# First norm's factor applied to the outputs of the query, key and value projections, inputs split without it, eight PSUM banks in that stage

## The reference, cut to what matters

```
x = rms_norm(hidden_states, ln_in_w)          # w * (x * rsqrt(mean(x*x) + 1e-6))
mixed = jnp.where(vm, x @ v_qkv, x @ l_qkv)   # vm: per token, which of two experts
q, k, v = jnp.split(mixed, 3, axis=-1)
q, k = apply_rotary(q, k, position_ids, l)
ctx = sdpa(q, k, v, causal=True)              # 16 heads of 32
```

## Time and profile before

| | |
|---|---|
| median of 3 runs | 2036.79 us (2032.74 to 2040.6) |
| profiled execution, its own time | 2036.72 us |
| its span, first to last instruction | 2034.9 us |
| granted TensorE clock, mean | 0.977 |
| PE busy | 1918.8 us, 94% |
| DVE, ACT, POOL busy | 1113.8, 830.2, 887.1 us |
| PE's first matmul / first product of the projections | 18.38 / 26.22 us |
| first scores of the self-attention | 138.29 us |

### The profile page before, as it was taken

One profiled execution on the slowest core, in us unless ns is written; L12 is line 12 of the kernel. 1 busy time (PEld: TensorE's weight loads), 2 busy tenths in 40 slices (PEclk: granted clock), 3 DMA queues, 4 the chain that ended last, 5 costly groups with the idle time before them and its releaser, 6 DMA issues.

```text
span 2034.9 us, 35472 instructions
## 1 busy us (share of the span) xinstructions
PE 1918.8 (94%) x12620; PEld 1642.6 (81%) x12620; DVE 1113.8 (55%) x2663; ACT 830.2 (41%) x2198; POOL 887.1 (44%) x1037
## 2 busy tenths in 40 slices
PE   4999979997999999999999999998979999999998
PEld 3876767775999989888899879985458888887997
DVE  6777875666442553547676554222384766655422
ACT  2017526875211211256666423222235666652321
POOL 3340322341798999641121348840044212104884
PEclk9999988999999999999999999998989999999999
DMA  3110100010233333310000213322221000001332
GB/s 127 42 57 2 40 15 16 30 50 17 83 109 109 115 114 124 88 35 18 11 24 13 67 63 104 114 73 88 70 80 34 19 10 24 13 1 42 104 113 79
DMA packets 38190, 118.88 MB, mean 58 GB/s; under 512 B 6168, under 2 KB 10264, under 8 KB 38016
## 3 DMA queue, kind: packets, MB, share of 16 engines
q1 hardware_dynamic: 31408, 107.92, 17.3%
q10 hardware_dynamic: 6608, 8.68, 1.4%
HBM read 114.75 MB, written 1.84 MB: 57 GB/s over the span
## 4 chain that ended last, share of the span: by engine, by line
PE 82%; DVE 7%; POOL 5%; ACT 2%; issue 2%; DMA 1%; DVEq 0%; ACTq 0%; SPq 0%; POOLq 0%
PE psum L565 15%; PE psum L566 14%; PE psum L567 14%; PE psum L787 7%; PE psum L798 6%; PE psum L845 5%; PE psum L558 4%; PE psum L685 4%; PE psum L687 4%; PE psum L686 4%; POOL wl L1701 3%; DVE xc L1277 1%; DVE rstd L1262 1%; ACT probs_t L1042 1%; DVE total L1248 1%
## 5 line engine op out<-in xcount | busy, mean ns | idle before, releaser
L1701 POOL TENSOR_TENSOR wl<-raw,wh 128x256 fp32r<-128x256 f32 x656 | 518.9, 822 | 13.7
L565 PE MATMUL psum<-nh,wh 128*128 128x448 f32 x904 | 348.3, 385 | 15.3 <-DVEq L1477 8.0
L1693 POOL TENSOR_SCALAR wh<-raw 128x1024 fp32r<-128x1024 f32 x164 | 185.1, 1129 | 396.8 <-PE psum L567 158.4
L566 PE MATMUL psum<-nl,wh 128*128 128x448 f32 x904 | 336.9, 373 | 0.0
L567 PE MATMUL psum<-nh,wl 128*128 128x448 f32 x904 | 336.3, 372 | 0.0
L1042 ACT ACTIVATE probs_t<-masked_t,nmin 112x375 f32<-112x375 f32 (+1 forms) x384 | 202.6, 529 | 109.2 <-DVE nmin L1380 109.2
L1549 DVE TENSOR_TENSOR hid_l<-scr,hid_h 128x448 fp32r<-128x448 f32 x108 | 93.2, 863 | 229.0 <-ACT hid_h L1129 228.4
L565 PEld LDWEIGHTS psum<-nh,wh 128*128 128x128 f32 x904 | 174.7, 193 | 37.6 <-issue 12.5
L1380 DVE CUSTOM_DVE_ANT_0 masked_t<-psum,maskf 112x375 f32<-112x375 f32 x256 | 129.7, 544 | 116.9 <-PE psum L787 116.2
L798 PE MATMUL psum<-cst,probs_t 112*125 112x112 f32 (+1 forms) x1304 | 188.4, 274 | 3.8 <-ACT probsT_t L1069 3.4
L1069 ACT COPY probsT_t<-psum 125x336 f32<-125x336 f32 (+1 forms) x424 | 175.5, 456 | 40.4 <-PE psum L845 23.4
(11 more groups left out here) (182 smaller groups left out, 3861.9 us busy)
## 6 DMA issues: line engine op xcount, KB each, us to landing
raw<-in_walls SPq DMA_DIRECT2D x183, 512.0 KB, 3.5
raw<-in_ctxF SPq DMA_DIRECT2D x24, 375.0 KB, 3.0
ctxb<-in_ctxF ACTq DMA_DIRECT2D x8, 375.0 KB, 3.6
ctxt<-in_ctxK ACTq DMA_DIRECT2D x8, 375.0 KB
x<-in_xT ACTq DMA_DIRECT2D x2, 896.0 KB, 11.2
outT<-x SPq DMA_DIRECT2D x2, 896.0 KB, 5.1
mask<-in_kmask ACTq DMA_DIRECT2D x16, 41.0 KB, 2.6
vself<-in_tt SPq DMA_DIRECT2D x1, 448.0 KB, 6.5
```

The lines of the kernel that those rows point to most:

```text
L565: nc.tensor.matmul(out, ah, bh, start=(i == 0), stop=False)
L566: nc.tensor.matmul(out, ah, bl, start=False, stop=False)
L1693: nc.gpsimd.tensor_scalar(high, src, 1.0, 1.0, ALU.mult, ALU.mult).then_inc(split_h, 1)
L1701: last = nc.gpsimd.tensor_tensor(low[cut], src[cut], high[cut].bitcast(F32), ALU.subtract)
```

## The change

1. The norm of this block no longer scales its input. New parts "x" (`X_PART`): for each slice ACT writes `nh_` as x*w, rounded, and squares x; DVE writes `nl_` as x*w - nh_ and adds the square to `total`. The products can start from these.
2. The factor, once its reciprocal is there, is multiplied into the masks: `vr0` (mask times factor, per expert) is used in `part_of` in place of `vm`, `vml` for queries and keys. For the values the factor is needed with tokens in partitions: four small matmuls per half with two columns (`total` times `mean_w`), a root into `std_t`, a reciprocal, and `vmT` is multiplied by it.
3. Order: half 0's part "x" comes first on ACT and DVE, ahead of positions, tables and token types; its variance and the tables come behind the first tile, half 1's part "x" behind them and its variance behind the second tile.
4. The stage has eight banks (`plan.use(range(8))`), the rotations lag by two tiles and have a counter of their own ("rope"); before the attention PE waits for the last readers of banks 3 to 7, and goes back to three.
5. Loads: the first weights are issued first on SP; the second half of x is issued once the first has landed; the waits for the constants move from the start of PE and GpSimd to where they are used.

```diff
+        vr0 = at("vr0", [P, 2, T], F32, o_k)
...
-            "qk": [("norm", 0, 0, "s"), ("norm", 0, 0, "v"), ("table",), ("norm", 0, 0, "f")] + qk_order(parts(0, 1, s=(0, 0, 0), v=(0, 0, 1), f=(0, 0, 1))),
+            "qk": [("norm", 0, 0, "x"), ("norm", 0, 0, "f")] +
+            qk_order(both({(0, 0, 0): [("norm", 0, 0, "v"), ("table",)]}, parts(0, 1, x=(0, 0, 0), v=(0, 0, 1), f=(0, 0, 1)))),
...
+                    pe.wait_ge(cst_in, 16)
-                    nc.tensor.matmul(pool_bank(n)[:, 0:HALF], mean_w, total[:, :], start=True, stop=True)\
-                        .then_inc(tile_ready, 1)
+                    last = nc.tensor.matmul(pool_bank(n)[:, 0:HALF], mean_w, total[:, :], start=True, stop=True)
+                    if nn == 0:
+                        for j in range(BPH):
+                            last = nc.tensor.matmul(pool_bank(n)[0:S, HALF + 2 * j:HALF + 2 * j + 2], total[:, bcols(j)],
+                                                    mean_w[:, 0:2], start=True, stop=True)
+                    last.then_inc(tile_ready, 1)
...
-                        if qk_seen[0] >= 1:
-                            rotate(qk_seen[0] - 1)
+                        if qk_seen[0] >= 2:
+                            rotate(qk_seen[0] - 2)
...
-            pe.wait_ge(cst_in, 16)
...
-                n = begin_tile(("rot", i), "dve")
+                n = begin_tile(("rot", i), "rope")
...
+            plan.use(range(8))
+            rotate(len(RAW) - 2)
...
+            plan.use(range(POOL))
+            for bank in range(POOL, 8):
+                bank_free(bank)
...
-                if part in S_PART:
+                if part in X_PART:
+                    x_whole(act, nn, half)
+                    act.wait_ge(vec_in, 16)
+                    for k in X_PART[part]:
+                        i = turn_of[nn, half] * KD + k
+                        nc.scalar.activation(nh_[:, k, hcols(half)], x[:, k, hcols(half)], ACT.Copy,
+                                             scale=vec[:, VECS.index(wname), k:k + 1]).then_inc(nhigh, 1)
+                        if i >= 2:
+                            act.wait_ge(sq_used, i - 1)
+                        nc.scalar.activation(sq[:, i % 2, :], x[:, k, hcols(half)], ACT.Square).then_inc(sq_ready, 1)
+                elif part in S_PART:
...
-                    nc.scalar.activation(std[:, :], bank[:, 0:HALF], ACT.Sqrt,
-                                         bias=eps[:, 0:1] if e == 1e-6 else eps[:, 1:2]).then_inc(emptied["act"], 1)
-                elif part[0] == "f" and nn != 5:
+                    ins = nc.scalar.activation(std[:, :], bank[:, 0:HALF], ACT.Sqrt,
+                                               bias=eps[:, 0:1] if e == 1e-6 else eps[:, 1:2])
+                    if nn == 0:
+                        ins = nc.scalar.activation(std_t[:, half * BPH:half * BPH + BPH], bank[0:S, HALF:HALF + 2 * BPH:2],
+                                                   ACT.Sqrt, bias=eps[0:S, 0:1])
+                    ins.then_inc(emptied["act"], 1)
+                elif part[0] == "f" and nn != 5 and nn not in LATE:
...
-                        act.wait_ge(nraw, split_turn[nn, half] * KD + k + 1)
+                        act.wait_ge(nraw, raw_turn[nn, half] * KD + k + 1)
...
-            for half in range(2):
-                act.dma_start(x[:, :, hcols(half)], xT[:, :, hcols(half)]).then_inc(x_in[half], 16)
+            act.dma_start(x[:, :, hcols(0)], xT[:, :, hcols(0)]).then_inc(x_in[0], 16)
+            act.wait_ge(x_in[0], 16)
+            act.dma_start(x[:, :, hcols(1)], xT[:, :, hcols(1)]).then_inc(x_in[1], 16)
...
-            act.wait_ge(vmT_done, 2)
+            act.wait_ge(vmT_done, 6)
...
+                elif part in X_PART:
+                    if part in ("x", "x0"):
+                        sum_free(nn, half, "v")
+                    x_whole(dve, nn, half)
+                    i = turn_of[nn, half] * KD
+                    for k in X_PART[part]:
+                        dve.wait_ge(nhigh, split_turn[nn, half] * KD + k + 1)
+                        nc.vector.scalar_tensor_tensor(nl_[:, k, cols], x[:, k, cols], w[:, k:k + 1],
+                                                       nh_[:, k, cols].bitcast(F32), ALU.mult, ALU.subtract)\
+                            .then_inc(normed, 1)
+                        dve.wait_ge(sq_ready, i + k + 1)
+                        if k == 0:
+                            ins = nc.vector.tensor_copy(total[:, :], sq[:, i % 2, :])
+                        else:
+                            dve.wait_ge(sq_used, i + k)
+                            ins = nc.vector.tensor_add(total[:, :], total[:, :], sq[:, (i + k) % 2, :])
+                        ins.then_inc(sq_used, 1)
+                    if part in ("x", "x3"):
+                        dve.wait_ge(sq_used, i + KD)
+                        dve.sem_inc(summed_up, 1)
...
+                elif part[0] in "rf" and nn in LATE:
+                    tile_done(dve, ("var", nn, half))
+                    if nn == 0:
+                        hb = slice(half * BPH, half * BPH + BPH)
+                        nc.vector.reciprocal(rstd_t[:, hb], std_t[:, hb]).then_inc(std_t_used, 1)
+                    own = rstd[:, :]
+                    nc.vector.reciprocal(own, std[:, :]).then_inc(std_used, 1)
+                    if nn == 0:
+                        dve.wait_ge(std_t_used, half + 1)
+                        for e in range(2):
+                            nc.vector.tensor_mul(vmT[:, e, hb], vmT[:, e, hb], rstd_t[:, hb]).then_inc(vmT_done, 1)
+                        dve.wait_ge(std_used, turn_of[nn, half] + 1)
+                        for e, v in enumerate((vm, vml)):
+                            n = link(nc.vector.tensor_mul(vr0[:, e, cols], rstd[:, :], v[:, half * BPH:(half + 1) * BPH, :]
+                                                          .rearrange("p b s -> p (b s)")))
+                        dve.wait_ge(chain, n)
...
+            dve.wait_ge(vec_in, 16)
+            norm_part(0, 0, "x")
...
-            dve.wait_ge(vec_in, 16)
-                mine = (vm, vml)[e][:, half * BPH:(half + 1) * BPH, :].rearrange("p b s -> p (b s)")
+                if name == "qk":
+                    mine = vr0[:, e, hcols(half)]
+                else:
+                    mine = (vm, vml)[e][:, half * BPH:(half + 1) * BPH, :].rearrange("p b s -> p (b s)")
...
-                nc.vector.tensor_mul(dst, bank, sin).then_inc(emptied["dve"], 1)
+                nc.vector.tensor_mul(dst, bank, sin).then_inc(emptied["rope"], 1)
-                dve.wait_ge(emptied["dve"], count)
+                dve.wait_ge(emptied["rope"], count)
...
-            stage("qk", qk)
+            stage("qk", qk, range(1, len(SEQ["qk"])))
+            dve.wait_ge(vmT_done, 6)
...
-            sp.dma_start(scr[0:S, 3, 0:S].bitcast(I32), pos.partition_broadcast(S)).then_inc(pos_in, 16)
-            sp.dma_start(cst[:, :], consts).then_inc(cst_in, 16)
-            sp.dma_start(vself[:, 0:T].bitcast(I32), tt.partition_broadcast(P)).then_inc(tt_in, 16)
-            sp.dma_start(scr[0:S, 2, 2 * B:4 * B].bitcast(I32), ttT).then_inc(ttT_in, 16)
...
+                if n == 0:
+                    sp.dma_start(cst[:, :], consts).then_inc(cst_in, 16)
+                    sp.dma_start(scr[0:S, 3, 0:S].bitcast(I32), pos.partition_broadcast(S)).then_inc(pos_in, 16)
+                    sp.dma_start(vself[:, 0:T].bitcast(I32), tt.partition_broadcast(P)).then_inc(tt_in, 16)
+                    sp.dma_start(scr[0:S, 2, 2 * B:4 * B].bitcast(I32), ttT).then_inc(ttT_in, 16)
```

More of the change, by code:

```diff
@@ L152 @@
 S_PART = {"s": range(KD), "s0": range(2), "s1": range(2, KD)}
+LATE = (0,)
+X_PART = {"x": range(KD), "x0": range(1), "x1": range(1, 2), "x2": range(2, 3), "x3": range(3, KD)}
 class PoolPlan:
@@ L159, in __init__ @@
         self.n = 0
-        self.count = {"act": 0, "dve": 0}
+        self.count = {"act": 0, "dve": 0, "rope": 0}
         self.tiles = {}
@@ L299, in build @@
         eps = sb("eps", [P, 2])
+        std_t = sb("std_t", [S, B])
+        rstd_t = sb("rstd_t", [S, B])
         o_a = place[0]
@@ L347, in build @@
         tile_ready = sem("tile_ready")
-        emptied = {"act": sem("emptied_act"), "dve": sem("emptied_dve")}
+        emptied = {"act": sem("emptied_act"), "dve": sem("emptied_dve"), "rope": sem("emptied_rope")}
         x_in = [sem(f"x_in{half}") for half in range(2)]
@@ L373, in build @@
         std_used = sem("std_used")
+        std_t_used = sem("std_t_used")
         normed = sem("normed")
@@ L393, in build @@
         split_turn = {key: i for i, key in enumerate([o for o in order if o[0] != 5])}
+        raw_turn = {key: i for i, key in enumerate([o for o in order if o[0] != 5 and o[0] not in LATE])}
         def norm_done(eng, nn, half, k=KD - 1):
@@ L474, in build @@
             for it in SEQ[name]:
-                if it[0] == "norm" and it[3] in ("a", "s", "s0"):
```

(12 more changed lines are left out.)

## The result

The changed kernel takes 2046.14 us in the median of 5 runs (2045.51 to 2048.92); the kernel before took 2036.79 beside it (5 runs, 2029.71 to 2040.60). The ratio is 1.0047, 95% interval 1.0029 to 1.0066: slower by about 9.6 us (5.9 to 13.4). The forecast was 2035.4. The profiled execution of after took 2045.77 us.

What follows compares the result with a forecast made beforehand. The matrix engine PE bounds the kernel, busy 1918.8 of 2034.9 us. A front gain of 6.1 and a tail loss of 4.8 gave -1.3 on 2036.7, so 2035.4 us, range 2027 to 2042.

Steps and rivals of the forecast that it cites:

- Edits that cost nothing: ... 64 bytes more of SBUF: Whole kernel: moved constants' wait, a third counter and 64 more bytes of SBUF were taken to cost nothing.
- The rival for a slower result: Half 1 variance after 42.7 us, DVE late at tile 2: front gain 2, tail loss 5.5, 2040 us; chance 0.22.
- Front part: Loading to fifth projection tile: first matmul at 13.8 us, fifth tile at 55.8 instead of 61.9, gain 6.1 us.
- the drain of 1.38 us: After ACT's first table load: left out as unseen in the trace; with it the sum would be +0.1 us.
- the token types: DVE ops after the positions, ahead of the factor: 5.5 us beside GpSimd, until 28.7; bounds 4 and 6.5.
- the 2.5 us taken from a shorter stretch: PE behind its idle wait for half 1's variance: 5.1 us at the lower clock, costing 2.5 us.
- Middle: Fifth tile to the tiles' end: nothing changes, PE full, 5.71 us per tile, DVE hidden at some 5.3.
- The rival in which DVE never catches up: Full stretch: PE stalls 0.1 to 1 us for each of 12 tiles, 2045 to 2050 us; chance 0.06.
- Tail: Tiles' end T to the attention's first scores: T + 13.0 against T + 8.2, a loss of 4.8 us.
- the wait for the banks: Before the attention: PE waits for ACT's scaling and DVE's combination of batch 0's values, 1.7 us with hops.
- Sum of the stage: Edited stage: front gain and tail loss, -6.1 + 4.8 = -1.3 us.
- within 0.5%: Whole kernel: chance 0.87 that the time differs from before by no more than about 0.5%, 10 us.

Runs made afterwards that it cites:

- e1_pad: The kernel before with only std_t and rstd_t allocated, unused, 64 bytes that move the tiles behind them: 2045.09 us, ratio 1.0032 to before.
- e6_hid64: The kernel before with hid_h and hid_l alone placed 64 bytes higher: 2044.10 us, ratio 1.0027 to before.
- e2_noshift: The changed kernel with std_t and rstd_t allocated behind probs_t, so that older tiles keep their addresses: 2038.69 us, ratio 1.0006 to before.
- e3_lag1: The changed kernel with rotations one tile behind instead of two, std_t and rstd_t left in place: 2042.62 us, ratio 1.0024 to before.
- e4_tail: The changed kernel without the address shift, rotations one tile behind, batch 0's value tiles in banks 0 to 2: 2032.66 us, ratio 0.9976 to before.
- e0_before_again: The kernel before, unchanged, run again for a second trace: 2035.26 us, ratio 0.9991 to before.

## Why the prediction was wrong, step by step

**The step that failed is "Edits that cost nothing: ... 64 bytes more of SBUF".** It was priced at nothing because the bytes were free, and their place was not asked after. e1_pad prices it at 6.5 us and e6_hid64 at 5.5, out of a loss of 9.6 (5.9 to 13.4). Some 3 us are left; the first scores are 0.9 us late, and the intervals are wide enough for the difference. With the placement undone (e2_noshift) the change takes 2038.69 us, 3.3 above the forecast and inside its range. The rival for a slower result named other causes (variance later than 42.7, DVE behind at tile 2); neither came.

**Front part: right in its places, 1.1 us too good.** x's first half landed as taken, about 10.2, and the issues behind it did hold up ACT, for 1.33 us (10.21 to 11.54; forecast 1.8). The timeline of ACT in after:

```profile
10.21 0.55 ACTq L1121 DMA_DIRECT2D x<-in_xT  x1
10.79 0.64 ACTq L1122 DMA_DIRECT2D gate_in<-in_gates  x1
11.54 1.28 ACT L991 ACT_TABLE_LOAD   x1 [11.54 <-issue]
12.84 0.67 ACT L991 ACTIVATE nh<-x,vec 128x448 fp32r<-128x448 f32 x1
```

Holding the second half back brought the first one no earlier (10.14 before, in the earlier trace rows). The copy starts 0.02 us behind the end of the table load, so the drain of 1.38 us that the Trainium skill gives ("ScalarE: Activation LUTs", "What ACT_TABLE_LOAD costs") is not seen here either.

DVE's order in after; of each group one row:

```profile
20.93 1.15 DVE L1293 TENSOR_TENSOR total<-total,sq 128x448 f32<-128x448 f32 x1
22.29 0.76 DVE L1526 CAST scr<-scr 112x112 f32<-112x112 int32 x1 [0.21 <-DVE total L1293]
...
25.89 0.62 DVE L1536 TENSOR_SCALAR vself<-vself 128x896 f32<-128x896 int32 x1
...
29.71 2.92 DVE L1326 RECIPROCAL rstd<-std 128x448 f32<-128x448 f32 x1
...
35.40 0.62 DVE L1588 TENSOR_TENSOR scr<-scr 128x448 f32<-128x448 f32 x1
...
39.82 0.62 DVE L1293 TENSOR_TENSOR total<-total,sq 128x448 f32<-128x448 f32 x1
```

The x part was done at 22.1 (forecast 21.8), tile 0 at 36.0 (35.6), the x part of half 1 at 40.4 (40.6). Two errors cancelled: the five position ops took 3.6 us beside GpSimd (forecast 1.4, from rows without it), and the token types 3.7 (forecast 5.5), as GpSimd was done at 25.9. PE's variance followed at 40.65 (40.6), after 8.26 us idle (7.5). From there to the fifth tile it took 16.3 us and not 15.2: the clock cost more than the 2.5 us taken from a shorter stretch. The window 40 to 60 has a granted clock of 0.78, so at levels 1 and 0.5 some 8.8 us at the lower one, not 5.1. Gain 5.0 instead of 6.1.

**Middle: right.** 60.0 of 60.0 us busy from 60 to 120 us, and the 5 us of the fifth tile arrive whole at 124.96. The rival in which DVE never catches up is out.

**Tail: right mechanism, a term too small.** T is the end of the tiles' matmuls. Forecast T + 13.0, measured T + 14.3 (139.23 - 124.96), a loss of 6.1 us instead of 4.8. Up to the sum of the last tile the working holds (T + 5.2 forecast; the rotation starts at T + 5.1). Behind it the last rotation and the 24 value matmuls were put at 5.9 us at full clock, but PE had idled 3.41 us, and they took 8.2, until 138.2: the window 120 to 140 has a clock of 0.91, some 3.6 us at the lower level. DVE's and ACT's last work on the values did stand in the way of the scores, as forecast, though only DVE's is late:

```profile
135.54 0.69 ACT L1138 ACTIVATE vtmp<-psum,vmT 112x512 f32<-112x512 f32 x1 [89.40 <-PE psum L883]
```

```profile
138.27 0.75 DVE L1435 SCALAR_TENSOR_TENSOR vself<-psum,vmT,vtmp 112x512 f32<-112x512 f32 x1 [3.35 <-PE psum L883]
```

Two runs take the terms away one by one. With the shorter lag (e3_lag1) the scores start at T + 9.6, so the longer one cost 4.7 us, its lower clock included (3.1 forecast, T + 8.2 to T + 11.3). With the value tiles moved as well (e4_tail) it is T + 8.2 again (124.12 to 132.31), so the wait for the banks cost 1.4 (1.7 forecast), and the 6 us of the front are kept.

**Sum of the stage.** Forecast -1.3 us; the trace of after gives +0.9, e2_noshift +1.2 (-2.2 to +4.9). That part of the forecast stands within its own range, and "within 0.5%" was also what the ratio came to (1.0047, with an interval that reaches over it). The time itself left the range because of the placement.

## What to carry to other kernels

Read the allocation of a diff as closely as its instructions: a new buffer ahead of others moves every tile behind it, and a kernel of nothing but that padding, timed beside the change, tells placement from work. When PE is busy all the time and still slower, count its instructions in a fixed window, or time whole stages, instead of looking for waits, and do it in two traces of the same kernel first, to know how far they differ by themselves. A stall that a change opens (here the half 1 variance) is worth removing by asking for the result later, before more buffers are spent to run up to it; and the cost of a stall of several us is the idle time and a stretch at the lower clock behind it.

## What the runs showed of the hardware that was not expected

- The pace of back-to-back 128x448 matmuls at a granted clock of 1.00 has more than one value, and it differs between executions of one kernel: 496 of them in before's window from 1240 to 1340 us, 489 in e0_before_again's. Where in SBUF the `hid` tiles lie decides how much of the time is spent at the slower one: 64 bytes on, the three MLP stages take 631.8 us in every trace, against 622.8 to 628.9 (e6_hid64, ratio 1.0027). 0, 256 and 512 bytes time alike, 32 is not measurably worse, 64 is slow, and so is everything moved by 128.
- It is not simply a price of reading the moved operand. With 64 bytes the products of `nh`, which did not move, slow down too (364 to 372 ns in the mean, L565 before and L581 after). Between 1885 and 2020 us the mean distance of two starts was 204.5 ns behind products of `hid` and 204.9 behind those of `nh` in after (200.6 and 201.9 in before), but 206.4 and 202.5 with all moved by 128 bytes, and 201.9 and 205.4 with `hid` moved by 32. What in the chip causes it is open.
- In the edited stage the kernels run at about 206 ns (120.21 to 124.96 in after: 23 matmuls in 4.75 us). There the `hid` tiles play no part; and a tile takes the 5.71 us of before; so there is more than one cause of the slower pace.
- Small DVE ops beside GpSimd's splits took 0.63 to 0.79 us where the same ones took 0.22 to 0.28 without.
- Eight matmul records of two columns took 0.86 us at full clock (26.11 in after) and 1.52 at the lower one (42.27).
